# Multi-query attention inside a fused layer: keys, swapped keys and values from one projection

## What is computed

```
q = (x @ Wq + bq).reshape(B, T, 16, 8)      # Wq 128x128
k = (x @ Wk + bk)[:, :, None, :]            # Wk 128x8, one head for all
v = (x @ Wv + bv)[:, :, None, :]            # Wv 128x8
rope(t) = concat([t1*cos + t2*sin, t1*sin - t2*cos])   # halves of 4
out = softmax(causal(rope(q) . rope(k) / sqrt(8))) . v, then @ Wo + bo
```

## Time and profile before

| | |
|---|---|
| median of 3 runs | 1711.6 us (1711.49 to 1711.8) |
| the profiled execution | 1711.74 us |
| its span (first to last instruction) | 1709.9 us |
| mean granted TensorE clock | 0.982 of full speed |
| TensorE matmuls | 1611.6 us busy, 7232 instructions |
| attention b | about 793 to 1172 us of the span |

### The profile page before, as it was taken

How to read it: one execution, slowest core, us unless ns; L and a number is a source line. 1 busy time by engine, 2 the same in 40 slices (tenths; PEclk the granted TensorE clock), 3 DMA queues, 4 the chain that set the end, 5 groups by cost and what they waited for, 6 DMA issues and landing times. The chain is left out here.

```text
span 1709.9 us, 24775 instructions
## 1 busy us (share of the span) xinstructions
PE 1611.6 (94%) x7232; PEld 1247.3 (73%) x7232; DVE 1073.3 (63%) x1871; ACT 1013.1 (59%) x1872; POOL 887.0 (52%) x793
## 2 busy tenths in 40 slices
PE   3689899999999999999999999988999999999998
PEld 2357677777777777886666666656888888888887
DVE  5685858687877777666676666643554554554544
ACT  2147546464747464655878787875565565565554
POOL 3678645464646454552787777773333333333332
PEclk8789999999999999999999999998999999999999
DMA  3045444343434443541000000012555555555553
GB/s 106 1 166 195 163 148 148 136 157 117 157 136 148 148 146 129 209 166 50 1 1 1 2 0 1 1 37 101 198 193 200 196 185 194 200 191 206 194 186 136
DMA packets 72548, 215.88 MB, mean 126 GB/s; under 512 B 7387, under 2 KB 20832, under 8 KB 72416
## 3 DMA queue, kind: packets, MB, share of 16 engines
q1 hardware_dynamic: 72416, 214.35, 36.2%
HBM read 199.64 MB, written 14.68 MB: 125 GB/s over the span
## 5 line engine op out<-in xcount | busy, mean ns | idle before, releaser
L567 POOL TENSOR_TENSOR ARENA_R<-ARENA,ARENA_R 128x512 fp32r<-128x512 f32 x256 | 343.7, 1343 | 601.4 <-ACT ARENA_R L561 600.8
L591 DVE TENSOR_TENSOR ARENA<-ARENA,pair 128x512 f32<-128x512 f32 x512 | 349.0, 682 | 446.4 <-PE pair L346 408.1
L551 ACT ACTIVATE ARENA<-bank 128x512 f32<-128x512 f32 x512 | 306.4, 598 | 486.8 <-PE bank L346 485.4
L344 PE MATMUL pair<-ARENA_R 128*128 128x512 f32 x1064 | 417.3, 392 | 12.6 <-POOL ARENA_R L480 6.5
L346 PE MATMUL pair<-ARENA_R 128*128 128x512 f32 x1064 | 414.6, 390 | 0.0
L345 PE MATMUL pair<-ARENA_R 128*128 128x512 f32 x1064 | 414.1, 389 | 0.0
L561 ACT ACTIVATE ARENA_R<-ARENA 128x512 fp32r<-128x512 f32 x512 | 319.6, 624 | 28.8 <-DVE ARENA L591 26.8
L920 POOL TENSOR_TENSOR ARENA_R<-ARENA,ARENA_R 128x512 fp32r<-128x512 f32 x192 | 249.6, 1315 | 79.6 <-ACT ARENA L1125 76.2
L344 PE MATMUL bank<-ARENA_R 128*128 128x512 f32 x568 | 242.2, 426 | 23.4 <-DVE ARENA L1615 18.2
L344 PEld LDWEIGHTS pair<-ARENA_R 128*128 128x128 f32 x1064 | 200.8, 189 | 63.3 <-POOL ARENA_R L480 8.6
L346 PEld LDWEIGHTS pair<-ARENA_R 128*128 128x128 f32 x1064 | 200.7, 189 | 42.5
(11 more groups left out here) (216 smaller groups left out, 2020.6 us busy)
## 6 DMA issues: line engine op xcount, KB each, us to landing
ARENA_R<-split_weights SPq DMA_DIRECT2D x360, 512.0 KB, 4.7
split_weights<-ARENA_R SPq DMA_DIRECT2D x24, 512.0 KB, 3.8
X<-in_L_attn_a_x_dram SPq DMA_DIRECT2D x8, 256.0 KB, 5.4
ARENA<-in_L_ffn_Wg_dram SPq DMA_DIRECT2D x8, 256.0 KB, 3.0
ARENA<-in_L_ffn_Wu_dram SPq DMA_DIRECT2D x8, 256.0 KB, 2.8
ARENA<-in_L_ffn_Wd_dram SPq DMA_DIRECT2D x8, 256.0 KB, 3.5
out_dram<-X SPq DMA_DIRECT2D x8, 256.0 KB, 4.2
CST<-in_tables_dram SPq DMA_DIRECT2D x1, 835.5 KB, 4.6
```

The costliest lines, as they stand in the source:

```text
L344: pe.matmul(dst, wh, xh, start=start, stop=False)
L551: act.activation(SG[:, c % 2, :], bank[c % 2], ACT.Silu).then_inc(F.sil, 1)
L567: eng.tensor_tensor(HL[:, G % FC, :], HF[:, G % FC, :], HH[:, G % FC, :].bitcast(F32), ALU.subtract).then_inc(lo_done(G)[0], 1)
L591: v.tensor_tensor(HF[:, c % FC, :], SG[:, c % 2, :], bank[2 + c % 2], ALU.mult).then_inc(F.mul, 1)
```

## The change

One projection with new weights takes the place of those for k and for swapped k and of the value product. Its columns 0 to 23 are the keys three times, 32 to 55 the swapped keys three times, 64 to 71 the values.

- `rope_k` makes two VectorE operations on 24 partitions at (0,10); the second reads rows 32 to 55 and writes rows 0 to 23. `take_v` copies all rows with the bias to VT at (1,0), now the last reader of bank 6.
- GpSimd's key sum (24 rows) moves from (1,1) to (0,11).
- `turn_v` at (1,3) transposes VT in four fp32 transposes; `split_v` reads columns 64 to 71 of each.
- The key stack is no product any more. ScalarE rounds the keys with a sign of -1 in rows 8 to 15 (`key_sign`) at (1,4); VectorE's `key_stack` at (1,5) computes `QK * key_lo + QKH` into rows 0 to 23 of group 0 in place of the subtraction for QKL; at (1,10) ScalarE copies group 0 from SBUF to the three other groups.
- The ramp is changed in the same way. One GpSimd memset of WB and one of the bias row are added, three table casts become one; the `khi` and `klo` tables go, two columns come. The value bias is loaded to BRAW in place of BB.

The diff cut to its core:

```diff
-            def project_v(nxt, subs):
-                pe.wait_ge(b_used[BPROJ[-1]], nxt.n + 1)
...
+            def turn_v(nxt):
+                pe.wait_ge(*b_read(nxt, "v"))
+                for k in range(SUB):
+                    m = pe.transpose(bank[6][:, k * P:(k + 1) * P], VT[:, k * P:(k + 1) * P], ident)
+                m.then_inc(B.v_ready, 1)
...
-            def key_stack(nxt):
-                pe.wait_ge(B.st_used, NJ * (nxt.n + 1))
-                pe.wait_ge(B.lo, 2 * (nxt.n + 1))
-                pe.matmul(bank[6], SELR[:, SK, :], QKH[:, 1, :], start=True, stop=False)
-                pe.matmul(bank[6], SELR[:, SKL, :], QKL[:, 1, :], start=False, stop=True).then_inc(B.kst_ready, 1)
...
-                        if b == 0 and k >= 5 and k % 2 == 1:
+                        if b == 0 and k in (5, 7, 9):
                             project_b(nxt, (k - 5) // 2)
-                        if b == 1 and k in (3, 4):
-                            project_v(nxt, range(2 * (k - 3), 2 * (k - 2)))
+                        if (b, k) == (1, 3):
+                            turn_v(nxt)
...
+            def rope_k(t):
+                v.wait_ge(*b_projected(t, "kv"))
+                after(v, B.u_k, t.n)
+                for at, table, dst in ((0, "cos_b", B1), (RG, "sin_b", B2)):
+                    rg = slice(at, at + 3 * DB)
+                    v.scalar_tensor_tensor(seqs(dst[0:3 * DB, 1, :]), seqs(bank[6][rg, :]), BQK[rg, 2:3],
+                                           spread(cst(table)[rg, :], SPT), ALU.add, ALU.mult).then_inc(b_used, 1)
+            def take_v(t):
+                after(v, B.v_ready, t.n)
+                v.tensor_scalar(VT[:, :], bank[6], BQK[:, 2:3], None, ALU.add).then_inc(b_used, 1)
...
+            def key_stack(nxt):
+                v.wait_ge(B.hi, 2 * nxt.n + 2)
+                after(v, B.t_ready, 2 * UNITS * (nxt.n - 1))
+                after(v, B.q2_ready, 4 * (nxt.n - 1))
+                rg = slice(0, 3 * DB)
+                v.scalar_tensor_tensor(KST[nxt.p][rg, 0, :], QK[rg, 1, :], cst("key_lo")[rg, :],
+                                       QKH[rg, 1, :].bitcast(F32), ALU.mult, ALU.add).then_inc(B.kst_ready, 1)
...
-                    if nxt.real() and (b, k) in ((0, 9), (1, 1)):
-                        rotated(nxt, 0 if b == 0 else 1)
+                    if nxt.real() and (b, k) in ((0, 9), (0, 11)):
+                        rotated(nxt, (k - 9) // 2)
...
-                    rg = slice(g * RG, g * RG + 3 * DB)
-                    act.activation(KST[nxt.p][rg, g, :], bank[6][rg, :], ACT.Copy).then_inc(B.kst_used, 1)
+                    act.activation(KST[nxt.p][g * RG:g * RG + 3 * DB, g, :], KST[nxt.p][0:3 * DB, 0, :].bitcast(F32),
+                                   ACT.Copy).then_inc(B.kst_used, 1)
...
-                    key_rows(nxt, range(NG))
+                    key_rows(nxt, range(1, NG))
```

More of the change, by code:

```diff
@@ L76, in constants @@
     c["pick"] = np.eye(P, 2, dtype=np.float32)
+    part = np.arange(P) // DB
+    c["key_lo"] = (part == 1).astype(np.float32)[:, None]
+    c["key_sign"] = np.where(part == 1, -1.0, 1.0)[:, None]
     inv = (1.0 / 10000.0 ** (np.arange(0, DB, 2, dtype=np.float32) / DB)).astype(np.float32)
@@ L268, in program @@
         RO = take(2, HB)
-        WB = take(4, P)
+        WB = take(3, P)
+        VT = take(TOK)
         WQB, WKB, WVB = take(C), take(DB), take(DB)
-        BRAW = take(C + DB)[0:1, :]
-        BQKR = take(4, C)[0:1, :, :]
+        BRAW = take(C + 2 * DB)[0:1, :]
+        BQKR = take(3, C)[0:1, :, :]
         STAGED = take(CWIDTH - CS)
-        BB = take(C + DB)
-        BBL = take(C + DB)
+        BB = take(C)
+        BBL = take(C)
         XTH = take(2, TOK, dt=F32R)
@@ L300, in program @@
         QKH = take(2, TOK, dt=F32R)
-        QKL = take(2, TOK, dt=F32R)
+        QKL = take(TOK, dt=F32R)
         VS = take(2, SUB, 2 * P - RG, dt=F32R)
@@ L832, in prep_stacks @@
                     g.tensor_copy(SELR[:, NJ + j, :], staged(f"qlo_{j}")).then_inc(pr.selr, 1)
-            def prep_keys():
-                for k, table in enumerate((staged("khi"), staged("klo"), ident)):
-                    g.tensor_copy(SELR[:, 2 * NJ + k, :], table).then_inc(pr.selr, 1)
             def prep_masks():
+                g.tensor_copy(SELR[:, 2 * NJ, :], ident).then_inc(pr.selr, 1)
                 for k, table in enumerate((staged("mask_rows"), staged("mask_cols"), ident)):
@@ L1065, in ramp @@
                     prepare(T0, 1, 5 + c - 20)
[L1066 removed]
+                if c in (24, 25, 26):
                     act.wait_ge(B.kst_ready, 1)
                     act.wait_ge(pr.zero, 6)
[L1069 removed]
+                    key_rows(T0, (c - 23,))
             act.wait_ge(pr.bmix, 2)
@@ L1714, in attn, with rope_q @@
                         weighted(t, 1)
-            def rope_b(t, k, name, table, dst, bias):
-                v.wait_ge(b_ready[name], t.n + 1)
-                after(v, (B.u_q, B.u_k)[k], t.n)
-                v.scalar_tensor_tensor(seqs(dst), seqs(bank[6]), bias, spread(cst(table), SPT), ALU.add,
-                                       ALU.mult).then_inc(b_used[name], 1)
-            def split_b(nxt, i):
-                v.wait_ge(B.hi, 2 * nxt.n + i + 1)
-                after(v, B.kst_ready, nxt.n)
-                v.tensor_tensor(QKL[:, i, :], QK[:, i, :], QKH[:, i, :].bitcast(F32), ALU.subtract).then_inc(B.lo, 1)
+            def rope_q(t, name, table, dst, i):
+                v.wait_ge(*b_projected(t, name))
+                after(v, B.u_q, t.n)
+                v.scalar_tensor_tensor(seqs(dst), seqs(bank[6]), BQK[:, i:i + 1], spread(cst(table), SPT), ALU.add,
+                                       ALU.mult).then_inc(b_used, 1)
@@ new lines, in split_q @@
+            def split_q(nxt):
+                v.wait_ge(B.hi, 2 * nxt.n + 1)
+                after(v, B.st_ready, NJ * nxt.n)
+                v.tensor_tensor(QKL[:, :], QK[:, 0, :], QKH[:, 0, :].bitcast(F32), ALU.subtract).then_inc(B.lo, 1)
+            def key_stack(nxt):
[5 more added lines that the diff above has]
+                                       QKH[rg, 1, :].bitcast(F32), ALU.mult, ALU.add).then_inc(B.kst_ready, 1)
@@ L1748, in ramp @@
                     v.wait_ge(ld.tables_b, 32)
-                    rope_b(T0, 0, "q", "cos_b", B1[:, 0, :], BQK[:, 0:1])
+                    rope_q(T0, "q", "cos_b", B1[:, 0, :], 0)
                 if c == 13:
-                    rope_b(T0, 0, "qs", "sin_b", B2[:, 0, :], BQK[:, 1:2])
+                    rope_q(T0, "qs", "sin_b", B2[:, 0, :], 1)
                 if c == 15:
-                    rope_b(T0, 1, "k", "cos_b", B1[:, 1, :], BQK[:, 2:3])
+                    rope_k(T0)
+                if c == 16:
+                    take_v(T0)
                 if c == 17:
-                    rope_b(T0, 1, "ks", "sin_b", B2[:, 1, :], BQK[:, 3:4])
+                    split_q(T0)
                 if c == 18:
-                    split_b(T0, 0)
-                if c == 19:
                     v.wait_ge(pr.zero, 4)
```

165 lines of the change are left out of this document (78 added, 87 removed).

## The result

The changed kernel takes 1720.1 us (median of 5 runs, 1717.4 to 1720.9) against 1711.6 of the kernel before: a ratio of 1.0047, with a 95% interval of 1.0036 to 1.0059. It is 8.5 us slower, where 1701.2 us were forecast, and lies outside the range of 1694 to 1708. Its profiled execution took 1720.9 us (span 1719.0, 9.1 more than before).

A forecast was written before the change was run, and what follows sets the result against it. TensorE was taken as the bound, busy 44.1 of 45.2 us per tile. Gains of 2.3 (ramp), 1.2 (tile 0), 5.0 (tiles 1 to 5) and 1.95 (tile 6) made 10.5 us off 1711.7: 1701.2 us, range 1694 to 1708.

The forecast's parts named there:

- Part 1, the ramp: Preparation of the first tile (T0) in the first phase's last feed-forward tile: 2.3 us saved on TensorE.
- Parts 2 and 3: Steady tiles: transposes replace value matmuls, gain 1.1 us; three key rows instead of four let exponentials start 0.8 us earlier.
- The longer price of a row: ScalarE's key-row copies: 0.61 us each without overlap was kept; 0.50 would gain a further 0.3 us per tile.
- Part 4, the second key operation: `rope_k`'s added VectorE operation, 0.66 to 0.81 us, said to be just hidden in 0.93 us of VectorE idle time.
- place A: Start of a tile's second sequence, where TensorE idles 0.50 us waiting for VectorE's swapped-key rotation.
- the third edit of part 4: GpSimd's key sum at (0,11) holds VectorE's L1800, so the wait at place A ends 0.9 us later.
- The saved 0.70 us: Swapped-key projection removed between output projection and stack of the maxima: TensorE only reaches an existing wait 0.70 us earlier.
- TensorE's clock falls at place A: Rival: idle time grows from 0.5 to some 2.1 us, each clock drop costs some 2.4 us; 1715.6 us, chance 0.05.
- no collision: Rival: GpSimd or VectorE slip past each other, tiles 1 to 5 gain 0.9 us more; 1696.7 us, chance 0.22.
- `take_v` held: Rival: the next GpSimd operation (1.27 us) holds the value copy too, five times; 1707.5 us, chance 0.06.
- second key operation exposed: Rival: `rope_k`'s added VectorE operation is not hidden, 0.66 us more in six tiles; 1705.2 us, chance 0.10.
- Nothing off the path in the attention stage: Rival: other engines fill the freed time, only the ramp's gain remains; 1709.4 us, chance 0.07.

The follow-up runs named there:

- Run 6: The kernel before with only VectorE's batch statistics moved from (0,11) to (1,1); 1707.5 us, ratio 0.9981.
- run 4: Run 1 with `take_v` moved ahead from (1,0) to (0,11) and VectorE's batch statistics moved from (0,11) to (1,1); 1700.0 us, ratio 0.9939.
- run 7: Run 1 with eight unused matmuls (1.9 us) ahead of TensorE's wait at place A in tiles 0 to 5; 1711.2 us, ratio 1.0002.
- run 5: run 4 with GpSimd's key sum at (1,0) instead of (1,1); 1693.9 us, ratio 0.9903, the fastest version.
- run 3: The kernel before with one GpSimd sum of the key sum's size added at (0,11), its result unused; 1730.6 us, ratio 1.0109.
- Run 1: The changed kernel with GpSimd's key sum put back from (0,11) to (1,1); 1718.4 us, ratio 1.0039.
- run 9: Run 1 with the projection of keys and values done a second time where the swapped-key projection stood; 1707.5 us, ratio 0.9977.
- run 8: run 4 with GpSimd's key sum at (0,11) as in the change; 1718.9 us, ratio 1.0039.
- run 11: run 5 with the batch statistics back at (0,11); 1700.7 us, ratio 0.9947.
- run 12: The changed kernel with only GpSimd's key sum moved, to (1,0); 1714.2 us, ratio 1.0027.
- run 2: The changed kernel with twelve unused matmuls (2.8 us) ahead of TensorE's wait at place A in tiles 0 to 5; 1711.6 us, ratio 1.0004.
- run 10: run 5 with `take_v` back at (1,0), where the change has it; 1697.4 us, ratio 0.9921.

## Why the prediction was wrong

**What held.** *Part 1, the ramp:* from the bias matmuls (L1341, then L1337) to the stage's first matmul are 54.55 us before and 52.17 after, a gain of 2.4; forecast 2.3. The stage began 3.5 us earlier; the other 1.1 was there before the ramp. Run 6, the kernel before but for the statistics, is 1.7 us ahead at the same place, so that part belongs to the execution. *Parts 2 and 3:* the four transposes take 0.35 us in run 4 (forecast 0.36), and TensorE's first matmul of a tile waits 0.2 us for key rows that take 1.94/3 = 0.65 us each in place of 0.61:

```profile
912.75 1.94 ACT L1018 ACTIVATE ARENA_R<-ARENA_R 24x512 fp32r<-24x512 f32 x3
```

That is run 7. The longer price of a row, without overlap, was the right one of the two. *Part 4, the second key operation:* in tiles 2 to 5 L1842 is still preceded by 0.17 to 0.19 us of idle time, so the operation is hidden there; `take_v` takes 0.74 us and is never held. Where place A is out of the way (runs 5 and 6), parts 2 and 3, with what comes through of the projection's 0.7, are worth 2.1 us per tile.

**Two steps failed:** the price of the key sum at (0,11), the third edit of part 4, and the term that the sum has for the clock, which is nothing.

*The collision was priced at one GpSimd operation, and it is two.* The text said that L1800 "ends at about 987.2 instead of 986.2", with the key sum. But the next subtraction stands ready by then. In the kernel before it starts 0.54 us behind the previous one; a key sum of 1.3 us between the two leaves no distance, and L1816 is held past the subtraction as well: 2.44 us, where 1.3 were forecast. Tile 6 was a fair model for one operation. Run 3 shows that the key sum does this by itself, with the projection in place (2.45 us). Idle time came to 3.3 us instead of the 2.1 forecast.

*The saved 0.70 us was followed on TensorE alone.* The prediction let it end in TensorE's own wait ("only arrives 0.70 us earlier at a wait it already has"). But the subtraction waits for exponentials that wait for TensorE's step (1,0), and this comes earlier without the swapped-key projection. Run 1 shows the effect without the key sum (distance 0.21 us, L1816 1.36 us), run 9 removes it by putting the work back (0.56 and 0.29 us). So putting the key sum back was not enough, though in the changed kernel the key sum alone makes the collision.

*The clock.* The rival "TensorE's clock falls at place A" is what happened, at a chance of 0.05. What was wrong is how the gap was placed: "The gap lies nearer to the harmless one" compared 2.1 us with the gap of tile 0 that left the clock alone (1.5 us in the window of the earlier trace rows, 1.71 us in all) and with the stage's longest, 6.17 us. The trace of the kernel before has one in between, in its first phase, with TensorE busy at a clock of 1.00 ahead of it:

```profile
168.39 0.50 PE L344 MATMUL pair<-ARENA_R 128*128 128x512 f32 x1 [2.36 <-POOL ARENA_R L480]
...
160.00:166.03 6.03, 6.03 (x27) 4.65 (x25) 2.65 (x3) 5.98 (x11) 5.88 (x7) 1.00 0.58 190
...
170.00:173.00 3.00, 3.00 (x9) 2.33 (x8) 1.53 (x9) 0.82 (x2) 2.92 (x4) 0.50 0.60 231
```

So 2.1 us lay nearer to a gap of 2.36 us behind which the clock fell, and the chance should have been several times as large. By runs 3, 8, 11 and 12 a gap of 1.5 us is harmless here in each of five tiles, one of 2.2 to 2.6 us goes either way, and at the 3.3 us of the changed kernel the clock fell in all five. The price of a fall, 2.4 us, was of the right size: 1.4 to 3.0 us each in runs 8 and 12, 1.9 per tile on average by run 2. That is partly luck: the "2 us at the lower level" were the length of the stretch that the earlier trace rows shows, and from 1146 to 1153 us the clock of that trace is 0.51 on average.

*The sum, remade.* For tiles 1 to 5 the forecast of -1.0 each is 1.1 + 0.8 + 0.7 = 2.6 us taken off and 1.6 of idle time added at place A (0.5 to 2.1). The trace shows +13.4 in five, +2.7 each. The idle time added is 2.8 (0.5 to 3.3), 1.2 above the forecast. The clock adds 1.9. And less than 2.6 was taken off: a tile without its idle time at place A is 45.25 - 0.50 = 44.75 before, 44.22 - 1.52 = 42.70 in run 11 and 43.56 - 0.88 = 42.68 in run 10, so some 2.05; which of the three terms was too large is not shown. That makes -2.05 + 2.8 + 1.9 = +2.65. In tile 0 the forecast was -1.2 and the trace shows +1.7. There TensorE waits twice in a short time (1.54 us before L1377 at 803.13, 1.86 before L1456 at 806.32; before, once, 1.71), which is 1.7 us more, and the clock falls too (run 2, where it holds, is 1.1 us shorter in this tile):

```profile
806.00:810.00 4.00, 3.68 (x15) 3.03 (x15) 1.55 (x4) 1.65 (x3) 0.00 (x0) 0.58 0.00 0
810.00:814.00 4.00, 4.00 (x14) 2.46 (x13) 2.24 (x4) 3.59 (x6) 1.89 (x3) 0.57 0.00 0
```

Tile 6, without statistics, has its collision once as before, idles 0.79 us, and gains 1.65 us where 1.95 were forecast.

The other rivals: *no collision* is refuted, in every tile with statistics; *`take_v` held* in all seven tiles (0.74 us); *second key operation exposed* outside tile 0. *Nothing off the path in the attention stage* is refuted by the first sequences (22.14 to 21.27 us) and by run 5. *VectorE's added work* as the cause is refuted by run 9, which has all of it. The chances of the first four add up to 0.88, not 0.87.

**The rule of the Trainium skill.** SBUF — State Buffer, section Who interferes with whom, has VectorE instructions with two SBUF inputs and reading GpSimd ones exclude each other for a whole instruction. The trace agrees on the pairing (L1816 held, the reductions and `take_v` from PSUM never) and on the whole instruction. The step went wrong in counting how many GpSimd instructions one VectorE instruction has to wait for.

## What to carry to other kernels

Work taken off the bounding engine makes everything it feeds come earlier too: before a saving ahead of a wait is called neutral, or an operation is moved into another engine's short gap, follow the other engines' next operations and see onto what they now fall; a distance of 0.3 us can be the reason that a wait is short. Where a wait of the matmul engine grows past the longest gap that the trace shows to be harmless, look through the whole trace for the shortest gap that was not, price the clock in every iteration with a large chance, and test it with a few useless matmuls in the gap. A short operation that can be held belongs behind work that can't be held, and long work nobody waits for (the statistics here) behind the wait: with the key sum moved out of the way, that turned +8.5 us into -17.6.

## What the runs showed of the hardware

- A pair of VectorE operations of 0.29 us took 1.3, 2.45 or 3.67 us beside one, two or three GpSimd operations without a gap between them. Whether a held VectorE operation gets in where two GpSimd operations follow at once depends on the place: between key sum and subtraction it never did (five tiles of the changed kernel, six of run 8), between subtraction and key sum one always did (L1813 ends at 897.02 in the changed kernel, behind the subtraction's 896.90 and long before the key sum's 898.13). Why is open.
- With the same idle time of 2.24 or 2.47 us the clock fell in some tiles and held in others of one execution; in run 3 it fell at 2.66 us in four tiles of four and held at 2.58 in one. Such a kernel's time is also less steady, and goes with its mean clock (0.980 at 1708.0 us, 0.969 at 1722.1 in run 12): 1708.0 to 1722.1 us in run 12, 1710.0 to 1722.3 in run 8, against 1699.9 to 1700.9 in run 4 and 1700.2 to 1703.1 in run 11.
- Matmuls whose results nobody reads, in the idle time, bought 8.5 us in run 2 and 7.2 in run 7.

Not tried: the change with `take_v` moved ahead and nothing else.
